# Recurrent mixer: parts of a chunk redistributed over sixteen steps, output projection moved to the second chunk behind

## The reference

```
delta = shift_by_one_token(x) - x
z     = tanh((x + delta * mu_x) @ W_x1.T)            # 5 groups of 32
mu_n  = z_n @ W_x2_n + x_bias_n                      # n = r, w, k, v, g
r, k, v, g = (x + delta * mu_n) @ W_n.T
w     = tanh((x + delta * mu_w) @ A_w.T) @ B_w.T + b_w ; w = -exp(w)
per token: o = r (S + u k v) ; S = exp(w) S + k v    # 4 heads, S is 32 x 64
o     = layernorm_per_head(o) * gn_weight + gn_bias
out   = (o * silu(g)) @ W_o.T
```

## Time and profile before

| | us |
|---|---|
| median of 3 runs | 3644.09 (3638.44 to 3647.27) |
| the profiled execution | 3638.03 |
| its span (first to last instruction) | 3636.2 |
| the mixer: start to its last residual add | about 0 to 865 |
| stages c = 1 to 14 (first mu matmul of each stage) | 98.38 to 811.5 |

### The profile page before, as it was taken

One profiled execution on the slowest core, in us unless ns is written; L12 is line 12 of the kernel. 1 busy time (PEld: TensorE's weight loads), 2 busy tenths in 40 slices (PEclk: granted clock), 3 DMA queues, 4 the chain that ended last, 5 costly groups with the idle time before them and its releaser, 6 DMA issues. The chain is left out here.

```text
span 3636.2 us, 78012 instructions
## 1 busy us (share of the span) xinstructions
PE 3315.7 (91%) x31460; PEld 1957.4 (54%) x31460; DVE 2503.2 (69%) x4755; ACT 2009.9 (55%) x2991; POOL 758.0 (21%) x887
## 2 busy tenths in 40 slices
PE   7999999995899939999999999999999999968998
PEld 4556555554677714444444444444444444427777
DVE  6676667663677717777767778687786776807776
ACT  3444444441555503666666667666676666755554
POOL 3444444342121110102011020110110201011112
PEclk8888888885999966999999999999999999989999
DMA  1000000001111142122222212122121312120110
GB/s 49 14 25 25 13 25 25 19 13 60 61 47 47 36 93 39 25 43 50 38 37 51 42 46 43 28 59 42 46 42 23 65 33 44 22 74 30 49 51 30
DMA packets 110471, 145.76 MB, mean 40 GB/s; under 512 B 21632, under 2 KB 94352, under 8 KB 109328
## 3 DMA queue, kind: packets, MB, share of 16 engines
q1 hardware_dynamic: 109344, 137.95, 16.1%
q0 software_dynamic: 768, 2.82, 0.4%
HBM read 53.99 MB, written 38.41 MB: 25 GB/s over the span
## 5 line engine op out<-in xcount | busy, mean ns | idle before, releaser
L1767 DVE TENSOR_REDUCE b_half_max<-banks 128x1 f32<-128x512 f32 x2048 | 1314.4, 685 | 443.2 <-PE banks L1492 261.6
L1718 ACT ACTIVATE b_p_t<-banks 128x1024 f32<-128x1024 f32 x1024 | 1047.0, 1025 | 397.3 <-PE banks L1492 256.0
L1548 PE MATMUL banks<-b_k_stack,b_q_stack 62*128 62x512 f32 x2048 | 828.9, 477 | 34.2 <-issue 17.8
L1609 PE MATMUL banks<-b_q_stack,b_k_stack 64*128 64x512 f32 x2048 | 851.7, 469 | 0.0
L1564 PE MATMUL banks<-b_p_t,b_v 128*17 128x256 f32 x8192 | 640.9, 385 | 25.1 <-ACT b_pv L1687 24.5
L1609 PEld LDWEIGHTS banks<-b_q_stack,b_k_stack 64*128 64x128 f32 x2048 | 342.9, 185 | 432.2 <-issue 416.7
L1492 PE MATMUL banks<-b_tables,b_halves 64*128 64x128 bf16 x4096 | 437.0, 224 | 0.0
L1548 PEld LDWEIGHTS banks<-b_k_stack,b_q_stack 62*128 62x128 f32 x2048 | 337.5, 188 | 68.6 <-issue 25.4
L1108 ACT ACTIVATE ffn_relu<-banks,ffn_scale_fc 128x512 f32<-128x512 f32 x256 | 176.3, 689 | 274.2 <-PE banks L1044 274.2
L1057 PE MATMUL banks<-ffn_proj_t,ffn_r_hi 128*128 128x256 f32 x1024 | 257.0, 285 | 2.5 <-DVE ffn_r_lo L1227 2.5
L1564 PEld LDWEIGHTS banks<-b_p_t,b_v 128*17 128x17 f32 x8192 | 135.9, 95 | 225.3 <-issue 76.6
(11 more groups left out here) (231 smaller groups left out, 4948.1 us busy)
## 6 DMA issues: line engine op xcount, KB each, us to landing
ffn_x<-x SPq DMA_DIRECT2D x32, 512.0 KB, 3.9
b_q_stack<-b_qk_hi SPq DMA_DIRECT2D x256, 64.0 KB
b_k_stack<-b_qk_hi SPq DMA_DIRECT2D x256, 64.0 KB
a_x<-hidden_states SPq DMA_DIRECT2D x16, 512.0 KB, 3.9
x<-a_x SPq DMA_DIRECT2D x16, 512.0 KB, 2.9
x<-ffn_x SPq DMA_DIRECT2D x16, 512.0 KB, 2.9
b_x<-x SPq DMA_DIRECT2D x8, 1024.0 KB, 5.6
b_k_stack<-b_qk_lo SPq DMA_DIRECT2D x128, 64.0 KB
```

The lines of the kernel that those rows point to most:

```text
L1548: last = pe.matmul(m, q_stack[rows, slot, qb * P:(qb + 1) * P], k_stack[rows, slot, half * BANK:(half + 1) * BANK], start=True, stop=not h ...
L1609: last = pe.matmul(out, k_stack[stack, slot, kb * P:(kb + 1) * P], q_stack[stack, slot, half * BANK:(half + 1) * BANK], start=True, stop=n ...
L1718: act.activation(p_t[use % P_BUFS][:, :, :], scores[use % 2], ACT.Exp, scale=slopes()[pair][0]).then_inc(p_made, 1)
L1767: dve.tensor_reduce(half_max[:, (pair + rg * PAIRS) * QB + qb, half:half + 1], misc.at["max", g, turn], axis=AX.X, op=ALU.max, negate=True ...
```

## The change

All parts but recur (8 steps) now have 16 steps, so that index k of one part stands beside index k of the others; step j of recur comes between indices 2j and 2j+1. Among equal indices the order is project_out, finish, prepare, normalize. The output projection becomes a part of its own, `project_out(c-2)`, in indices 0 to 3 of the stage after the one where it stood, and there is one more stage. Within an index PE now has: 0: y0, mu pair 0; products 0; 1: y1, mu pair 2; 2: y2; products 1; 3: y3, low, mu pair 4; 4: w, r, mu pair 6; advance 0; 5: xt0; 6: k, xt1; products 2; 7: mu pair 8; 8: v0; advance 1; 9: v1; 10: transposes of o; products 3; 11: g0; 12: g1, z0; advance 2; 13: z1; advance 3. The square of o on ACT comes at index 3, the sum on DVE and the power on POOL at 5, the scaling on DVE at 8, the gate on POOL at 12. POOL's additions of x stand at 5 (k's, behind the power), 6 (v's) and 9 (g's, inside the tree). The moments of the next chunk's layernorm are taken at index 14 of the stage before.

The diff, with unchanged lines left out:

```diff
...
-        NORMALIZE, PREPARE, RECUR, FINISH = 7, 14, 8, 12
+        STEPS, RECUR = 16, 8
...
-        def schedule(recur, finish, prepare, normalize):
-            for c in range(-2, CHUNKS + 1):
+        def steps(n):
+            for _ in range(n):
+                yield
+
+        def schedule(recur, project_out, finish, prepare, normalize):
+            for c in range(-2, CHUNKS + 2):
...
-                             *([(FINISH, finish(c - 1), 1)] if c > 0 else []),
-                             *([(PREPARE, prepare(c + 1), 1)] if 0 <= c + 1 < CHUNKS else []),
-                             *([(NORMALIZE, normalize(c + 2), 1)] if c + 2 < CHUNKS else []))
+                             *([(STEPS, project_out(c - 2), 1)] if c > 1 else []),
+                             *([(STEPS, finish(c - 1), 1)] if 0 < c <= CHUNKS else []),
+                             *([(STEPS, prepare(c + 1), 1)] if 0 <= c + 1 < CHUNKS else []),
+                             *([(STEPS, normalize(c + 2), 1)] if c + 2 < CHUNKS else []))
...
         def tensor(pe):
             def normalize(c):
...
-                yield
-                yield
+                yield from steps(5)
...
-                    if kt == 0:
-                        yield
-                yield
-                yield
+                    yield
+                yield from steps(5)
...
+                yield from steps(2)
             def prepare(c):
...
-                for turn in (0, 2, 4, 6):
+                for turn in (0, 2):
...
+                yield
...
-                mix_in(8)
+                mix_in(4)
...
+                mix_in(6)
+                yield
...
+                mix_in(8)
+                yield
...
+                yield
...
-                for _ in range(TREE - 4):
-                    yield
+                yield from steps(3)
             def recur(c):
...
             def finish(c):
...
-                for _ in range(4):
-                    yield
+                yield from steps(10)
...
-                for _ in range(3):
-                    yield
+                yield from steps(6)
+
+            def project_out(c):
...
+                yield from steps(12)
...
-            for c in schedule(recur, finish, prepare, normalize):
+            for c in schedule(recur, project_out, finish, prepare, normalize):
...
         def scalar(act):
             def normalize(c):
...
-                yield
-                yield
+                yield from steps(5)
...
-                    if kt == 0:
-                        yield
-                yield
-                yield
+                    yield
+                yield from steps(5)
...
+                yield from steps(2)
             def used_up(c):
...
-                for _ in range(4):
-                    yield
+                yield from steps(3)
...
+                yield
...
+                next(levels)
+                yield
...
+                    next(levels)
...
+                    yield
+                next(levels)
+                yield
+                for m in range(KT):
...
-                    yield
-                for m in range(KT):
...
-                    next(levels)
-                    yield
-                yield from levels
+                    yield
+                next(levels)
+                yield from steps(3)
             def carry(c):
...
             def finish(c):
...
+                yield from steps(3)
...
-                for _ in range(4):
-                    yield
+                yield from steps(7)
...
-                for _ in range(FINISH - 4):
-                    yield
+                yield from steps(6)
+
+            def project_out(c):
+                yield from steps(STEPS)
...
-            for c in schedule(recur, finish, prepare, normalize):
+            for c in schedule(recur, project_out, finish, prepare, normalize):
...
         def vector(dve):
-            def normalize(c):
-                par, x = c % 2, xs[c % X_BUFS]
-                xt, delta = xn_t[par], deltas[par]
+            def take_moments(c):
+                x = xs[c % X_BUFS]
...
-                yield
+
+            def normalize(c):
+                par, x = c % 2, xs[c % X_BUFS]
+                xt, delta = xn_t[par], deltas[par]
+                if c == 0:
+                    take_moments(c)
+                yield from steps(4)
...
-                yield
-                yield
-                yield
+                yield from steps(5)
...
-                yield
-                yield
-                yield
+                yield from steps(5)
+                if c + 1 < CHUNKS:
+                    take_moments(c + 1)
+                yield from steps(2)
             def prepare(c):
...
-                for i, (j, kt) in enumerate(MIXED):
-                    n, (used, value) = ORDER[j], mix_free(c, j)
-                    if kt == 0 and value:
-                        dve.wait_ge(used, value)
-                    dve.wait_ge(mu_ready, 10 * c + i + 1)
-                    dve.scalar_tensor_tensor(out=mix(j)[:, kt, :], in0=ring.at["mu", c, j, kt], scalar=x_bias[:, n, kt:kt + 1],
-                                             in1=delta[:, kt, :], op0=ALU.add, op1=ALU.mult).then_inc(mu_scaled, 1)
-                    if i == 3:
-                        for own in range(2):
-                            dve.wait_ge(mu_scaled, 10 * c + SCALED[own])
-                            dve.tensor_tensor(mix(own)[:, :, :], mix(own)[:, :, :], xt[:, :, 1:], ALU.add).then_inc(first_mixes, 1)
-                    if i % 2:
-                        yield
-                yield
-                yield
-                for _ in range(2):
+                def mix_in(turn):
+                    for i in (turn, turn + 1):
+                        j, kt = MIXED[i]
+                        n, (used, value) = ORDER[j], mix_free(c, j)
+                        if kt == 0 and value:
+                            dve.wait_ge(used, value)
+                        dve.wait_ge(mu_ready, 10 * c + i + 1)
+                        dve.scalar_tensor_tensor(out=mix(j)[:, kt, :], in0=ring.at["mu", c, j, kt], scalar=x_bias[:, n, kt:kt + 1],
+                                                 in1=delta[:, kt, :], op0=ALU.add, op1=ALU.mult).then_inc(mu_scaled, 1)
+
+                mix_in(0)
+                yield
+                mix_in(2)
+                for own in range(2):
+                    dve.wait_ge(mu_scaled, 10 * c + SCALED[own])
+                    dve.tensor_tensor(mix(own)[:, :, :], mix(own)[:, :, :], xt[:, :, 1:], ALU.add).then_inc(first_mixes, 1)
+                yield
+                yield
+                mix_in(4)
+                yield
+                mix_in(6)
+                yield from steps(3)
+                next(levels)
+                mix_in(8)
+                yield
+                for _ in range(4):
...
+                    next(levels)
...
-                    next(levels)
-                    yield
-                yield from levels
+                    yield
+                yield from steps(2)
             def carry(c):
...
             def finish(c):
-                o, x = o_bufs[c % 2], xs[c % X_BUFS]
+                o = o_bufs[c % 2]
...
-                yield
+                yield from steps(5)
...
-                yield
-                yield
+                yield from steps(3)
...
-                for _ in range(4):
-                    yield
+                yield from steps(8)
+
+            def project_out(c):
+                x = xs[c % X_BUFS]
...
+                yield from steps(12)
             def get_ready():
...
-            for c in schedule(recur, finish, prepare, normalize):
+            for c in schedule(recur, project_out, finish, prepare, normalize):
...
         def gpsimd(pool):
-            def normalize(c):
-                xt = xn_t[c % 2]
+            def take_rstd(c):
...
-                yield
-                yield
-                yield
+
+            def normalize(c):
+                xt = xn_t[c % 2]
+                if c == 0:
+                    take_rstd(c)
+                yield from steps(6)
...
-                for _ in range(4):
-                    yield
+                yield from steps(8)
+                if c + 1 < CHUNKS:
+                    take_rstd(c + 1)
+                yield from steps(2)
             def prepare(c):
...
-                for _ in range(3):
-                    yield
-                for j in range(2, MIXES):
+                def add(j):
...
-                    yield
-                yield
-                yield from levels
+
+                yield from steps(5)
+                add(2)
+                yield
+                add(3)
+                yield
+                for l in range(TREE):
+                    next(levels)
+                    if l == 2:
+                        add(4)
+                    yield
+                yield from steps(2)
             def carry(c):
...
```

(13 more changed lines are left out.)

## The result

The changed kernel takes 3809.28 us (median of 4 runs, 3803.03 to 3811.65) against 3641.27 for the kernel before, measured beside it: a ratio of 1.0456, 95% interval 1.0441 to 1.0471. It is slower, as forecast, and by more: 168 us instead of 111. The profiled execution took 3811.61 us with a span of 3809.8, against 3638.03 and 3636.2: +173.6.

A forecast was written before the change was run, and what follows sets the result against it. Bound: the mixer, each stage a VectorE-led part at low clock, then gapless TensorE work. 16.1 + 3.0 + 10.4 + 4.5 + 20.8 = 54.8, with 4.6 for clock 59.4 us a stage against 51.3; 3755 us, range 3680 to 3830.

The forecast's parts named there:

- The first wait, at w: From y0 to low's tanh on ACT, 16.1 us; TensorE has 13.0 us of work and waits 3 us.
- The second wait, at k: From mu pair 6 through DVE's and POOL's queues to k, 10.4 us, of which TensorE idles 7.3.
- The clock: TensorE's clock falls in both waits and is low when it starts again: 4.6 us a stage, bounds 0 to 12.
- The two groups that I priced: Matmuls behind the waits at low clock: w and r up to 3.0 us more, k and xt1 up to 2.3.
- The rest: From products 2 to the stage's end: 20.2 us of TensorE work plus 0.6 of waits, 20.8.
- Head: 0: The start of the mixer, ahead of the full stages, was to cost nothing more.
- Tail: End of the mixer: chunk 14's y's leave stage 15 (-3) and run at low clock (7), +4 us.
- (b): Rival, no change: only the chain at k costs and the clock holds, 51.6 us a stage, 3646 us; chance 0.07.
- (c): Rival: clock stays low from the second wait to v0, 66.8 us a stage, 3853 us; chance 0.17 with (d).
- (d): Rival: clock still falls in a stage's first third, 65.4 us a stage, 3834 us; chance 0.17 with (c).
- (a): Rival, faster: low clock goes and neither wait decides, stage 44.3 plus about 1 us, 3555 us; chance 0.10.
- The kind of matmul: On TensorE in the old order, the clock depends on the kind of matmul too, not only on idling.

The follow-up runs named there:

- e3: Changed kernel with low's tanh one step earlier on ScalarE, ahead of the placing and the square: 3758.10 us, 1.0304 of the kernel before.
- e7: Changed kernel with mu pairs 4 and 6 one step earlier on TensorE and VectorE: 3773.36 us, 1.0363 of the kernel before.
- e1: Changed kernel with the root one step later on POOL, behind k's addition: 3761.74 us, 1.0326 of the kernel before.
- e11: Changed kernel with the moves of e1, e3 and e7 together: 3618.38 us, 0.9941 of the kernel before.
- e9: Changed kernel with matmuls of constants put into TensorE's waits ahead of w, k and g, nothing moved: 3752.59 us, 1.0305 of the kernel before.
- e5: Changed kernel with output projection and finishing work back where the kernel before has them, mixes still spread: 3748.26 us, 1.0297 of the kernel before.
- e10: e4 with g's addition one tree level earlier on POOL and nothing else: 3762.05 us, 1.0323 of the kernel before.
- e8: Changed kernel with e1, e3 and e7, plus VectorE's normalizing multiplication in step 2 and g's addition one tree level earlier: 3724.68 us, 1.0231 of the kernel before.
- e4: Changed kernel with the moves of e2 and e3 together: 3676.57 us, 1.0090 of the kernel before.
- e2: Changed kernel with VectorE's sum of squares, POOL's root and k's addition one step earlier: 3750.78 us, 1.0299 of the kernel before.

## Why the prediction was right, and where its size was off

*The first wait, at w*, "16.1": 488.78 to 505.17 is 16.4, with 2.79 us of waiting for the tanh behind the square. e3 took away the wait with the tanh alone. Right.

*The second wait, at k*, "from the start of mu pair 6 to k: 10.4": 510.77 to 521.33 is 10.6. Mix, xn, sum, root and addition stand in the timelines in that order. Right in size, incomplete in cause: "I see nothing that could take this chain apart" overlooked that the sum waits for the state update as well. e7 shows it; e1 with e7 and e3, in e11, takes the chain apart.

*The clock*, "I take 4.6": low behind the two waits as said, w and r 5.6 us instead of 3.0, k to products 2 5.9 instead of 4.5, and a third fall at g, its first half 3.2 instead of 1.8 us. The two groups that I priced cost 4.0, the third 1.4. That is 5.4, and e9 gives 5.0 by another way. So the size is near, in part because a fall that I did not have makes up for two that I put somewhat too high.

*The rest*, "0 to 1.7 of waits, 0.6 taken": the step that failed within a stage. It is 1.5 to 1.7, in each stage, and the fall at g hangs on it: 23.2 us instead of 20.8. POOL adds g's mix inside the tree, with the addition at 2.98 us beside VectorE's mixed_x. Together 61.65 us where I had 59.4, so 10.3 and not 8.1 a stage: 133.8 us where the forecast has 105 for these thirteen stages. That is half of the miss.

*"Head: 0"*: the other step that failed, 21 us. I had priced only stages with a recurrence and a finish behind them. In stage -1 there is neither, so each link of mixes, tanh and additions that the spreading stretched is a bare wait: TensorE waits 4.7 us for xn (slowed to 4.36 us beside two POOL additions) and 1.6 for g's mix, and has neither of these waits in the kernel before; a wait of 3.1 for the mix ahead of low stands in both. In stage 0 the waits for the placing, k and g take 6.3 us where one of 1.0 stood, and the clock is 0.76 instead of 0.81. e5 (42.4 and 58.6 us for the two) shows that the spreading does this and not the moved projection.

*Tail*: with stage 14, 15.1 us instead of the 9 in the forecast; I did not take it apart, beyond e5, which gets 11 of them back with the projection.

*The rivals.* (b) fell: w had a wait of its own and the clock did not hold. (c) did not happen in this order, and (d) only in the stages 0 and 1, which have no y's; but both are real: e10's low clock runs from the end of one stage through 19 us of light matmuls of the next, at 62.35 us a stage. (a) had TensorE's work in a stage right, though not for this order: e11's stage at full clock holds 47.9 - 3.8 us of waits = 44.1 us of work, against my 44.3.

*The kind of matmul*: that it "matters too" holds for the kernel before; the section on the hardware shows a fall there that no wait precedes.

Left open: why the clock in e8 and e11 falls in some stages and not in others with the same waits, and the 11 us that e11's head still costs. g's wait of 1.7 was not taken out of e11.

## What to carry to other kernels

When a change moves steps of several engines, write down for the new order each queue around each handover, and follow every operation back through all that stands ahead of it in its own queue, not only to its inputs: here a root that served a later step stood in front of an addition that the next matmul needed, and a state update in front of the root's sum. A wait of TensorE costs itself and what the clock does behind it, so put unavoidable waits ahead of full-size matmuls rather than ahead of a stretch of small ones (e10 against e4 is the one case here that shows it). Price the first stages by themselves: a pipeline that is spread out has nothing beside it there.

## What the runs showed of the hardware

**VectorE and GpSimd block each other.** xn: 1.37 us alone (changed kernel, above), 2.62 beside POOL's addition (e2, above). It began 0.50 us behind the addition and lost 1.25 of the 1.50 us that this had left. A tree product of 0.28 us took 2.08 in e10, where the addition ran beside it until 554.68:

```profile
552.75 2.08 DVE L696 TENSOR_TENSOR a_decay<-a_decay 128x128 f32<-128x128 f32 x1
```

```profile
552.51 2.17 POOL L816 TENSOR_TENSOR a_mix<-a_mix,a_xn_t 128x1024 f32<-128x1024 f32 x1
```

The scaling of o was 2.57 us in the kernel before, beside the addition at 475.07, and 1.21 in the changed one with POOL quiet: its low price there is a gain of the change that I had not counted. The Trainium skill (SBUF — State Buffer, Who interferes with whom) says that the two share a port pair, that a VectorE instruction with two inputs in SBUF contends with a GpSimd instruction that reads SBUF, and that so does tensor_scalar (xn here) in a mode that uses both ports, where the first to issue holds the pair for its whole instruction. The trace agrees with a contention in these cases.

**The price of TensorE's clock depends on what follows a wait.** 2.4 us of waits at the end of e10's stage are followed by some 24 us at 1.2 GHz across the boundary, and the next stage, with its second fall, is 8.65 us longer; in the changed kernel 11 us of waits in three places gave 17 us at the low level and cost 5.0. The Trainium skill (TensorE: Matmul & The Clock Gate, Part 1) explains the falls by idling, and e9 agrees: with the waits filled PEclk is 1.00. It does not explain why a TensorE that is busy with small matmuls stays low, as in the earlier trace rows and in e8's stage at 0.79, which was busy for 55.70 of its 59.84 us, nor that the clock can fall before any wait. Windows of stage 1 of the kernel before, cut where the clock fell:

```profile
98.38:101.50 3.12, 2.94 (x103) 1.98 (x105) 1.67 (x3) 1.94 (x4) 0.81 (x2) 1.00 0.02 5
101.50:118.60 17.10, 15.88 (x177) 8.81 (x172) 16.03 (x34) 4.17 (x12) 6.37 (x5) 0.50 0.01 1
```

TensorE ran a mu pair and pair products ahead of the fall, busy for 2.94 of 3.12 us, and came to the stage without a gap; the wait of 0.98 us for the placing ends only at 105.14. So in the kernel before not only the wait lowers the clock. And the mean clock over the thirteen stages was 0.85 in the kernel before and 0.85 in the changed one, 134 us apart: the mean alone does not tell what an order loses.
